# A scatter's wait, the x sums' number format and the one-hots' instruction, changed in the sort and node stages of a graph network

## The reference

```python
# gated layer
msg = x[src] @ W_msg.T + b_msg + edge_embed[clip(edge_type, 0, 8)]
x = layernorm(x + gru(segment_sum(msg, dst), x))

# three layers, self loops added; ei[0] is src, ei[1] is dst, so the sums are by SOURCE node
ee = ea @ enc_w + enc_b
h = x[ei[1]] + ee                      # layer 0; layers 1 and 2: concat([x[ei[1]], ee])
agg = segment_sum(h, ei[0])
h = relu(bn(agg @ w1 + b1)) @ w2 + b2
...
x = layernorm(x + h)
```

## Time and profile before

| what | value |
| --- | --- |
| median of 3 runs | 6228.43 us (6224.02 to 6235.12) |
| span of the profiled execution | 6981.5 us (the page has no other time for it) |
| instructions in it | 88118 |
| TensorE matmul, busy | 5386.3 us, 77% |
| GpSimd, busy | 4213.9 us, 60% |
| VectorE, busy | 3769.9 us, 54% |
| ScalarE, busy | 3302.5 us, 47% |
| TensorE weight loads (beside matmuls) | 3361.9 us, 48% |
| DMA | 1066 MB, mean 153 GB/s |

### The profile page before, as it was taken

One profiled execution on the slowest core, in us unless ns is written; L12 is line 12 of the kernel. 1 busy time (PEld: TensorE's weight loads), 2 busy tenths in 40 slices (PEclk: granted clock), 3 DMA queues, 4 the chain that ended last, 5 costly groups with the idle time before them and its releaser, 6 DMA issues.

```text
span 6981.5 us, 88118 instructions
## 1 busy us (share of the span) xinstructions
PE 5386.3 (77%) x26429; PEld 3361.9 (48%) x26429; DVE 3769.9 (54%) x14165; ACT 3302.5 (47%) x4432; POOL 4213.9 (60%) x4243
## 2 busy tenths in 40 slices
PE   4376767676766764666676999999898998898998
PEld 1133333333333322333344666666666666666666
DVE  8576767777766754455566444443333333444443
ACT  1164545555655641122122666665555554554554
POOL 5655555555555556666631666666676666666665
PEclk5588988888988985677776999999999999999999
DMA  7165556556655652333323666667666667666665
GB/s 250 48 144 129 140 121 138 127 134 136 157 127 127 148 138 76 98 101 102 100 78 121 188 190 185 194 196 220 184 186 179 190 191 217 184 184 174 177 185 148
DMA packets 1068177, 1066.40 MB, mean 153 GB/s; under 512 B 494051, under 2 KB 784501, under 8 KB 1067701
## 3 DMA queue, kind: packets, MB, share of 16 engines
q1 hardware_dynamic: 889573, 782.05, 40.1%
q0 software_dynamic: 178128, 278.65, 16.0%
HBM read 747.21 MB, written 216.68 MB: 138 GB/s over the span
## 4 chain that ended last, share of the span: by engine, by line
PE 44%; another core or an unknown queue 6%; DVE 4%; issue 4%; ACT 2%; DMA 1%; SPq 0%; DVEq 0%; ACTq 0%
PE ps L2965 27%; PE ps L2935 4%; PE ps L2848 2%; PE ps L2899 2%; PE ps L2809 2%; PE ps L2810 1%; DVE BIG L2197 1%; PE ps L2909 1%; PE ps L2910 1%; PE ps L2811 1%; ACT MSR L2575 1%; DVE MSR L2258 0%; PE ps L2812 0%; PE ps L2914 0%
## 5 line engine op out<-in xcount | busy, mean ns | idle before, releaser
L3051 POOL DMA_INDIRECT GL<-h_gathered,IDXA x2058 | 2112.6, 1027 | 1227.7 <-issue 568.5
L2965 PE MATMUL ps<-MSR,HP 128*128 128x512 f32 (+1 forms) x9000 | 2375.0, 410 | 174.9 <-ACT MSR L2575 71.2
L3017 POOL DMA_INDIRECT rec_q<-BIG x1563 | 1513.7, 968 | 1156.2 <-issue 473.6
L2575 ACT CAST MSR<-MS 128x1024 fp32r<-128x1024 uint8 (+1 forms) x1500 | 1491.8, 1028 | 1272.9 <-PE ps L2965 820.3
L2965 PEld LDWEIGHTS ps<-MSR,HP 128*128 128x128 f32 x9000 | 1675.6, 195 | 624.9 <-issue 168.5
L2750 PE MATMUL ps<-MTB,XPS 128*128 128x512 bf16 x4410 | 1312.2, 416 | 1.1 <-DMA XPS<-x_parts 0.8
L2258 DVE CAST MSR<-MS 128x1024 fp32r<-128x1024 uint8 (+1 forms) x750 | 522.6, 699 | 1236.7 <-PE ps L2965 738.5
L2457 ACT CAST MT<-ps 128x512 uint16<-128x512 f32 x735 | 427.4, 582 | 959.2 <-remote 633.3
L2461 ACT CAST MTB<-MT 128x1024 bf16<-128x1024 uint8 x735 | 767.9, 1045 | 64.8 <-PE ps L2750 10.3
L3033 POOL DMA_INDIRECT BIG<-x_parts,SRCq x611 | 582.8, 954 | 341.5 <-issue 164.4
L2750 PEld LDWEIGHTS ps<-MTB,XPS 128*128 128x128 bf16 x4410 | 439.7, 103 | 248.7 <-issue 68.1
(11 more groups left out here) (248 smaller groups left out, 6244.4 us busy)
## 6 DMA issues: line engine op xcount, KB each, us to landing
MS<-counts SPq DMA_DIRECT2D x1080, 256.0 KB
counts<-BIG SPq DMA_DIRECT2D x360, 256.0 KB
XPS<-x_parts SPq DMA_DIRECT2D x192, 384.0 KB
GL<-h_gathered,IDXA POOLq DMA_INDIRECT x2058
rec_q<-BIG POOLq DMA_INDIRECT x1563
rec_q<-BIG SPq DMA_DIRECT2D x44, 490.0 KB, 10.4
HTI<-h_cols SPq DMA_DIRECT2D x72, 256.0 KB
h_dense<-PCL SPq DMA_DIRECT2D x30, 512.0 KB
```

What stands on the lines that cost most here:

```text
L2575: s.copy(MSR[:, g % RM, :, 0:w].rearrange("p t (c s) -> p t c s", s=P), MSB[:, i % MR, 0:4 * w].rearrange("p (c h s t) -> p h t c s", h=2, ...
L2965: got = t.matmul(bank[:, 0:w], HP[:, d, part, :], MSR[:, g % RM, d % 2, 0:w], start=d + part == 0, stop=lay > 0 and d + part == BD, skip_g ...
L3017: g.indirect_dma_start(out=RAd, out_offset=bass.IndirectOffsetOnAxis(ap=POSI[:, c:c + 1], axis=0), in_=RECA[q % 3][:, c - a, :], in_offset ...
L3051: g.indirect_dma_start(out=GL[:, r % LR, i, 0:3 * P], out_offset=None, in_=HGd[lay], in_offset=bass.IndirectOffsetOnAxis(ap=IDXA[:, a + i: ...
```

## The change

There are four edits.

1. **Scatters.** The wait for landings stands at the first scatter of a four instead of its second, and is for the four before the last one.
2. **x sums.** x stands as two float32r parts (XR) instead of three bf16 parts for these sums: the first is x copied to float32r, the second what is left. They go to an array of their own in memory (XRd), the loads of XPS take 512 KB instead of 384, the counts are widened to float32r, and a cell has two matmuls instead of three. The three bf16 parts are made and stored as before, since the gathers use them.
3. **One-hots of a unit.** All source one-hots of a unit are made by one tensor_tensor, which compares BIN256 (the numbers 0 to 255, each four times) with the unit's four source keys, spread over the columns. The tile in the innermost place is the cell: column b of cell i stands at 4 b + i. The destination one-hots lose the weight; a second tensor_tensor multiplies the source one-hots by the weights (OHW), and the counts' matmul takes these. The ring of source one-hots has three places instead of four, and TensorE reads its weights with a step of four.
4. **Node stage.** The four destination one-hots of a group are one tensor_tensor in the same layout, and TensorE reads these with a step of four too.

Two waits are new beside the one moved: the weights' preparation on VectorE waits for the last x sum (their memory is shared now), and ScalarE waits once, at the first unit, for the stored x parts. The buffers Y, PC, XR, RT and XMT lie in the memory of MTB and XPS, which are used later.

The diff, cut to its core:

```diff
+        XRd = nc.dram_tensor("x_parts_wide", (NP, 2 * P), F32).ap()
...
-        DREL = sb("DREL", [P, C], F32, front)
+        DREL = sb("DREL", [P, C], F16, front)
...
-        IO256 = sb("IO256", [P, 256], F16, front)
+        BIN256 = sb("BIN256", [P, 256, GT], F16, front)
+        MTB = sb("MTB", [P, 3, 2048], F32R, cells)
+        XPS = sb("XPS", [P, 3, 4, 2, P], F32R, cells)
...
-        MTB = sb("MTB", [P, 3, 2048], BF16, front)
-        XPS = sb("XPS", [P, 3, 4, 3, P], BF16, front)
+        OHWT = sb("OHW", [P, 2, P, GT], BF16, front)
...
+        SRK = [big(4 * HU).bitcast(F16).rearrange("p (j c) -> p j c", j=2) for _ in range(2)]
-        OHS = [t(GT * 66).bitcast(BF16).rearrange("p (c b) -> p c b", b=132) for t in (big, big, big, more)]
+        OHS = [big(GT * 64).bitcast(BF16).rearrange("p (b c) -> p b c", c=GT) for _ in range(3)]
+        OHW = [OHWT[:, i, :, :] for i in range(2)] + [more(GT * 64).bitcast(BF16).rearrange("p (b c) -> p b c", c=GT)]
...
         def x_rest(v, i):
+            v.tensor_tensor(XR[:, i % 2, 0:n, 1, :], Y[:, i % 2, 0:n, :], XR[:, i % 2, 0:n, 0, :].bitcast(F32), ALU.subtract)
             v.tensor_tensor(RT[:, 0:n, :], Y[:, i % 2, 0:n, :], PC[:, i % 2, 0:n, 0, :], ALU.subtract).then_inc(*rest1.inc())
...
         def cells_vector(v, m):
+                v.tensor_copy(SRK[k % 2][:, 0:js, 0:w], RECS[k % 2][:, 0:js, 0:w, 1]).then_inc(*dve.inc())
...
-            if m >= 4:
-                v.wait_ge(mt.sem, pairs_to(m - 4))
-            for i in range(x.n):
-                got = v.tensor_scalar(OHS[m % 4][:, i, :], I132[:, :, 0:44], RECS[k % 2][:, par, x.at + i, 1:2], None, ALU.is_equal)
-            got.then_inc(*ohs.inc())
+            if m >= 3:
+                v.wait_ge(mt.sem, pairs_to(m - 3))
+            def keys(of):
+                return of[k % 2][:, par, x.at:x.at + x.n].unsqueeze(1).broadcast_to([P, P, x.n])
+            src = OHS[m % 3][:, :, 0:x.n]
+            v.tensor_tensor(src, BIN256[:, 0:P, 0:x.n], keys(SRK), ALU.is_equal).then_inc(*ohs.inc())
             for i in range(x.n):
...
-                v.tensor_scalar(OHD[c % 12], I258[:, :, 0:86], DSK[k % 2][:, par, x.at + i:x.at + i + 1],
-                                DSW[k % 2][:, par, x.at + i:x.at + i + 1], ALU.is_equal, ALU.mult).then_inc(*ohd.inc())
+                v.tensor_scalar(OHD[c % 12], I258[:, :, 0:86], DSK[k % 2][:, par, x.at + i:x.at + i + 1], None,
+                                ALU.is_equal).then_inc(*ohd.inc())
+            v.wait_ge(ohs.sem, m + 1)
+            v.tensor_tensor(OHW[m % 3][:, :, 0:x.n], src, keys(DSW), ALU.mult).then_inc(*ohw.inc())
...
         def weights_vector(v):
+            v.wait_ge(xd.sem, len(CELLS))
...
         def first_onehots(v, q, hot, types):
-            for i in range(n):
-                got = v.tensor_scalar(hot[:, i, :], IO256[:, :], DREL[:, GT * q + i:GT * q + i + 1], None, ALU.is_equal)
-            got.then_inc(*q0_hot.inc())
+            v.tensor_tensor(hot[:, :, 0:n], BIN256[:, :, 0:n], DREL[:, GT * q:GT * q + n].unsqueeze(1).broadcast_to([P, 256, n]),
+                            ALU.is_equal).then_inc(*q0_hot.inc())
...
         def x_high(s, i):
+            s.copy(XR[:, i % 2, 0:n, 0, :], Y[:, i % 2, 0:n, :])
             s.copy(PC[:, i % 2, 0:n, 0, :], Y[:, i % 2, 0:n, :]).then_inc(*part1.inc())
...
-                got = t.matmul(PS[4 + n % 2][:, 51 * i:51 * (i + 1)], OHS[m % 4][:, i, 0:P],
+                got = t.matmul(PS[4 + n % 2][:, 51 * i:51 * (i + 1)], OHS[m % 3][:, :, i],
...
+                if i == 0:
+                    t.wait_ge(ohw.sem, m + 1)
-                got = t.matmul(PS[PAIR[c // 2 % 2]][:, 256 * (c % 2):256 * (c % 2 + 1)], OHS[m % 4][:, i, 0:P], OHD[c % 12][:, 0:256],
+                got = t.matmul(PS[PAIR[c // 2 % 2]][:, 256 * (c % 2):256 * (c % 2 + 1)], OHW[m % 3][:, :, i], OHD[c % 12][:, 0:256],
...
-            for part in range(3):
+            for part in range(2):
                 got = t.matmul(PS[6 + x.j % 2][:, :], XPS[:, x.load % 3, i, part, :], MTB[:, m % 3, 512 * i:512 * (i + 1)],
...
-                        got = t.matmul(PS[5][:, 9 * (b % TC):9 * (b % TC) + 9], SXD[:, r, i, P * half:P * (half + 1)], OTD[:, r, i, 0:9],
+                        got = t.matmul(PS[5][:, 9 * (b % TC):9 * (b % TC) + 9], SXD[:, r, P * half:P * (half + 1), i], OTD[:, r, i, 0:9],
...
-                        got = t.matmul(PS[b % 3][:, 0:393], SX[:, r, i, P * half:P * (half + 1)], XG[:, r, i, 0:393],
+                        got = t.matmul(PS[b % 3][:, 0:393], SX[:, r, P * half:P * (half + 1), i], XG[:, r, i, 0:393],
...
-                    if quad and (c - a) % GT == 1:
-                        g.wait_ge(scat[q % 3][(quad - 1) % 2].sem, scattered_to(q, quad - 1))
+                    if quad >= 2 and (c - a) % GT == 0:
+                        g.wait_ge(scat[q % 3][quad % 2].sem, scattered_to(q, quad - 2))
...
-            y.dma_start(XPS[:, k % 3, 0:n, :, :].rearrange("p b a f -> p b (a f)"),
-                        XPd[512 * u:512 * u + P * n, :].rearrange("(b p) f -> p b f", p=P)).then_inc(*xps_in[k % 3].inc(16))
+            y.dma_start(XPS[:, k % 3, 0:n, :, :].rearrange("p b a f -> p b (a f)").bitcast(F32),
+                        XRd[512 * u:512 * u + P * n, :].rearrange("(b p) f -> p b f", p=P)).then_inc(*xps_in[k % 3].inc(16))
...
+            y.dma_start(XRd[512 * i:512 * i + P * n, :].rearrange("(b p) f -> p b f", p=P),
+                        XRW[:, i % 2, 0:256 * n].rearrange("p (b f) -> p b f", f=2 * P)).then_inc(*xp_out[i % 2].inc(16))
```

More of the change, by code:

```diff
@@ L1632, in program @@
         WMT = sb("WMT", [P, P], F32, front)
-        IO256 = sb("IO256", [P, 256], F16, front)
-        XMT = sb("XMT", [P, 2, 2 * P], F32, front)
-        Y = sb("Y", [P, 2, 4, P], F32, front)
-        PCW = sb("PC", [P, 2, 1024], F32, front)
+        BIN256 = sb("BIN256", [P, 256, GT], F16, front)
+        cells = ExitStack()
+        MTB = sb("MTB", [P, 3, 2048], F32R, cells)
+        XPS = sb("XPS", [P, 3, 4, 2, P], F32R, cells)
+        cells.close()
+        MTBW = sb("MTBW", [P, 3 * 2048], F32, front)
+        XPSW = sb("XPSW", [P, 3 * 4 * 2 * P], F32, front)
+        Y = MTBW[:, 0:1024].rearrange("p (q b f) -> p q b f", q=2, b=4)
+        PCW = MTBW[:, 1024:3072].rearrange("p (q c) -> p q c", q=2)
+        XRW = MTBW[:, 3072:5120].rearrange("p (q c) -> p q c", q=2)
+        XR = XRW.bitcast(F32R).rearrange("p q (b a f) -> p q b a f", b=4, a=2)
+        XMT = XPSW[:, 2560:3072].rearrange("p (q c) -> p q c", q=2)
+        RT = XPSW[:, 2048:2560].rearrange("p (b f) -> p b f", b=4)
         PC = PCW[:, :, 0:768].bitcast(BF16).rearrange("p q (b a f) -> p q b a f", b=4, a=3)
@@ L1687, in program @@
         DSK = [big(8 * HU).rearrange("p (j c) -> p j c", j=2) for _ in range(2)]
-        DSW = [big(8 * HU).rearrange("p (j c) -> p j c", j=2) for _ in range(2)]
+        DSW = [big(4 * HU).bitcast(F16).rearrange("p (j c) -> p j c", j=2) for _ in range(2)]
+        SRK = [big(4 * HU).bitcast(F16).rearrange("p (j c) -> p j c", j=2) for _ in range(2)]
         EAS = [big(2 * 20 * 51 // 2).bitcast(BF16).rearrange("p (j c a k) -> p j c a k", j=2, a=3, k=17) for _ in range(2)]
         more = carve(WE)
-        OHS = [t(GT * 66).bitcast(BF16).rearrange("p (c b) -> p c b", b=132) for t in (big, big, big, more)]
+        OHS = [big(GT * 64).bitcast(BF16).rearrange("p (b c) -> p b c", c=GT) for _ in range(3)]
+        OHW = [OHWT[:, i, :, :] for i in range(2)] + [more(GT * 64).bitcast(BF16).rearrange("p (b c) -> p b c", c=GT)]
         OHD = [t(129).bitcast(BF16) for t in (big,) * 8 + (more,) * 4]
@@ L1706, in program @@
         XG = ring(QR * GT * XW // 2).bitcast(BF16).rearrange("p (q i w) -> p q i w", q=QR, i=GT)
-        SX = ring(QR * GT * 128).bitcast(BF16).rearrange("p (q i w) -> p q i w", q=QR, i=GT)
-        SXD = ring(DR * GT * 128).bitcast(BF16).rearrange("p (q i w) -> p q i w", q=DR, i=GT)
+        SX = ring(QR * GT * 128).bitcast(BF16).rearrange("p (q w i) -> p q w i", q=QR, i=GT)
+        SXD = ring(DR * GT * 128).bitcast(BF16).rearrange("p (q w i) -> p q w i", q=DR, i=GT)
         OTD = ring(DR * GT * 8).bitcast(BF16).rearrange("p (q i w) -> p q i w", q=DR, i=GT)
@@ L1763, in program @@
         ohs = sem("cell_src")
+        ohw = sem("cell_src_weighted")
         ohd = sem("cell_dst")
@@ L2195, in first_onehots @@
             n = tiles_of(q, C)
-            for i in range(n):
-                got = v.tensor_scalar(hot[:, i, :], IO256[:, :], DREL[:, GT * q + i:GT * q + i + 1], None, ALU.is_equal)
-            got.then_inc(*q0_hot.inc())
-            v.tensor_tensor(types[:, 0:n, :], IO256[:, 0:9].unsqueeze(1).broadcast_to([P, n, 9]),
+            v.tensor_tensor(hot[:, :, 0:n], BIN256[:, :, 0:n], DREL[:, GT * q:GT * q + n].unsqueeze(1).broadcast_to([P, 256, n]),
+                            ALU.is_equal).then_inc(*q0_hot.inc())
+            v.tensor_tensor(types[:, 0:n, :], IOTH[:, 0:9].unsqueeze(1).broadcast_to([P, n, 9]),
```

(8 more changed lines are left out.)

20 lines of the change are left out of this document (8 added, 12 removed).

## The result

The changed kernel takes 5941.95 us (median of 4; 5936.31 to 5951.03) against 6230.41 beside it: a ratio of 0.9536, 95% interval 0.9513 to 0.9558. That is 288 us less where 190 were forecast, and 13 us under the lower end of the range.

What follows compares the result with a forecast made beforehand. GpSimd's scatters, with landing waits on the path, were taken to set the front's end, ahead of VectorE. Scatters -221, hold-up +30 and node stage 0 gave -191, rounded to -190: 6228.43 - 190 = 6038 us, range 5955 to 6175.

Steps and rivals of the forecast that it cites:

- Without the last two, 2675 - 422 = 2253: Front: with GpSimd's waits for VectorE (products 213, places 209 us) taken out, its last scatter comes at 2253 us.
- Gain 261 - 40 = 221 us: Scatters: moving the wait removes GpSimd's 261 us of landing waits, except 40 us; ends 0 and 261.
- the 40 us left for later landings: Scatters: 40 us of landing waits kept, for landings that come later because the DMA engines get more to do.
- The short stretches: Front: stretches of 41 us with VectorE busy 98 to 99%, taken as undisturbed, beside 62 us ones with nearly the same work.
- Rival 2: Front: landing waits are longer than their mean, worth up to 100 us more; about 5950 us, chance 0.10.
- priced the same way it is 0.893 us, so 0: Node stage: one instruction of 1024 elements costs VectorE the 0.893 us of the four it replaces; gain 0.
- ends from VectorE's share of the stage: Node stage: 0.60 and 1.34 us an instruction, times 395 groups and VectorE's share 635/1123: -66 to +100 us.
- The hold-up in the front: Cells: 750 new two-input VectorE instructions hold up GpSimd's scatters, 0.04 us each, 30 us on the path.
- price 0. If that cover goes, 17 us: x sums before the cells: extra copies and subtractions, 15 and 17 us, lie hidden beside the first three windows' scatters.
- 1: Rival: transfers take the gain, landings come late and two thirds of the waits stay; about 6150 us, chance 0.17.
- 3: Rival: the new tensor_tensor run at the float32 pace, 0.672 us, 1.34 in the node stage; about 6195 us, chance 0.08.
- 4: Rival: node stage weight loads at a step take 0.186 us, costing PE 271 us; about 6309 us, chance 0.08.

Runs made afterwards that it cites:

- first record: The profile of the unchanged kernel before that the prediction read; its span is 6981.5 us, 753 us above the median of the runs shown.
- second record: The kernel before, unchanged, recorded once more for a profile without the long stretches; it took 6228.87 us, its record 6225.9.

## Why the prediction was wrong, point by point

**The step that failed** is the first: "Without the last two, 2675 - 422 = 2253", and with it "Gain 261 - 40 = 221 us". The mechanism was right: GpSimd is the later engine, its landing waits lie on the path, moving the wait removes nearly all of them (the 40 us left for later landings are 33), and the issue pace is late next, with VectorE as full beside it. The term was mis-sized: the landing waits are 410 us, not 261, and moving the wait took 377 of them away and 364 us off the time. In the first record GpSimd waited 422 us for VectorE. I took these waits out as the recording's own, rightly, but kept the landing waits as they stood, as if the two were independent. By stages, the first record is 271 us longer than the second in the front (2677 to 2406), 169 in the node stage and 316 in the layers: taking 422 us out of the front and putting nothing back was 151 us too much, about what the landing waits lacked. That scatters land while GpSimd waits for something else, and that the record so hid 149 us of landing waits, is how I read the two records; it was not tried by itself.

With it fell the reading of the earlier trace rows. The short stretches, VectorE at 98 to 99%, are not the kernel's normal pace: the second record has VectorE at 84% from 700 to 1100. Rival 2, which took one short stretch at its word, had the direction and 100 of the 143 us that were missing in that term. That its 5950 us lies 8 us from the measured time is luck: it lacked the other 43, and some 40 of cost elsewhere.

**The node stage** was the second step: "priced the same way it is 0.893 us, so 0", with ends from VectorE's share of the stage. The instruction takes 0.680 us, and VectorE's 75 us less are worth nothing; the stage runs at GpSimd's gathers, and the new instruction holds them up. The prediction had the hold-up's price at hand and asked for it only in the front. By its own formula, (0.680 - 0.13)^2 / (2 x 1.256) is 0.12 us each, 39 us for the 322 that lie beside gathers in the changed kernel's trace (the expectation above took 312); measured 39 us of gathers, 34 of the stage.

**The hold-up in the front** was right: 30 us forecast, and undoing the cells' one-hots took 26 us from the scatters. VectorE: DVE Perf Modes, of the Trainium skill, in the section on the perf-mode tier table, gave an estimate of 424 ns for the new instruction; the trace has 414 and 410. SBUF — State Buffer, of the Trainium skill, in the section on who interferes with whom, would have a hold of the instruction's whole length, an estimate of 59 us by the prediction's sum and 50 with the durations measured; the trace has 26, which is the sum with the 0.13 us taken off.

**The x sums**: "price 0. If that cover goes, 17 us". The cover was not there: 14 us by the 65th scatter. The prediction looked only at the end of the third window, but GpSimd waits for places long before that. Two float32r matmuls also save less than forecast, 2 x 0.352 against 3 x 0.276 us a cell (1034.3/2940, and 1218.9/4410 in the second record of before), 0.125 instead of 0.366; that stayed hidden.

**The sum**, by the spans of the records (6225.9 to 5934.4, -292): the wait -364 in the front, then +36 there (14 and 13 of it found by undoing the cells' one-hots and the x sums, the other 9 not separated; three records with this front end it at 2075 to 2081, so each of these is sure to some 6 us) and +34 in the node stage; 2 us lie in the layers. In the other order the wait is worth 395 us (6336.58 to 5941.95) and the rest costs 102, since with the old wait it also adds to the landing waits. Two errors of opposite sign, 143 us too little for the wait and some 40 too little for the rest, gave a forecast some 100 us off. The prediction's 1.264 us for a scatter and its issue is 1.258 by the two numbers that it names, which moves nothing.

**The rivals**: 1 falls, landing waits are 31.5 us at a DMA share of 0.81. 3 falls, 0.41 us. 4 falls in its price: a weight load of line 2857 is busy 0.050 us (95.9/1912) against 0.044, under the 0.143 from which it would decide.

## What to carry to other kernels

Where an engine waits for the batch just before, look first at what stands between issue and landing: one batch more in flight was worth 6% here, and the other three parts of the change together cost 1%. When one wait is taken out of a record, waits of other kinds on the same engine need not stay as they are; check a record whose span is far from the timed runs against a second one before a sum rests on it. And an instruction that is cheaper on its own engine can have a price on an engine beside it: ask for it in every stage where the instruction stands.

## What the runs showed of the hardware

How sharply a two-input instruction holds an indirect DMA's issue: in the changed kernel 168 gathers began inside one of the node stage's new instructions; 106 of them took over 1.1 us, and these end 0.819 us after it (median; 0.814 to 0.837 from end to end). For the 46 scatters that began inside one of the cells' instructions and took over 1.1 us it is 0.829 us (median; a tenth lies above 0.833). Alone a gather takes 0.946 us (median), so some 0.13 us of it pass before it needs what is held. An issue that begins u us into an instruction of d us is then late by d - 0.13 - u; the mean over random starts is (d - 0.13)^2 / (2 x period), which three runs bear out for d of 0.41 and 0.68 us: 26, 17 and 39 us measured against some 24, 21 and 39. The one-input instructions that these replace leave the gathers at their 954 ns. Reading weights at a step of four columns cost 14 ns a load in the node stage (106 to 120 ns in the means of line 2834, second record of before, and line 2857; 106 again where this stage was undone), and 16 and 29 ns in the cells (lines 2725 and 2733: 101 to 117 and 130).
